# Rows of 272 columns in place of 258 for the first layer's gathered tokens

## What is computed

```
xn = layernorm(x)
x  = x + attention(xn) + ffn(xn)
```

## Time and profile before

| | |
|---|---|
| median of three runs | 1185.54 us |
| lowest, highest | 1183.62, 1187.75 us |
| profiled execution, its own time | 1182.18 us |
| its span, first to last instruction | 1180.4 us |
| mean granted TensorE clock | 0.956 |
| PE, DVE, ACT, POOL busy | 87%, 65%, 51%, 27% |
| share of the 16 DMA engines, queue of SP | 24.5% |
| the same, queue of POOL | 7.2% |

### The profile page before, as it was taken

How to read it: one execution, slowest core, us unless ns; L and a number is a source line. 1 busy time by engine, 2 the same in 40 slices (tenths; PEclk the granted TensorE clock), 3 DMA queues, 4 the chain that set the end, 5 groups by cost and what they waited for, 6 DMA issues and landing times.

```text
span 1180.4 us, 17538 instructions
## 1 busy us (share of the span) xinstructions
PE 1031.3 (87%) x5780; PEld 744.3 (63%) x5780; DVE 764.5 (65%) x1591; ACT 606.1 (51%) x911; POOL 317.1 (27%) x331
## 2 busy tenths in 40 slices
PE   4979697578999938699998999999999997999996
PEld 3867576467999924455454555555555555888885
DVE  6585254446665525789888878888888837444438
ACT  6325244246555543356665665666656665544431
POOL 2003678125674420000000011221221000455442
PEclk9999899789999969799999999999999998999999
DMA  6862233344444354012111113221222206333243
GB/s 229 311 269 81 94 110 123 104 130 128 154 128 130 117 213 143 7 31 33 17 29 27 27 48 61 54 64 41 59 59 59 65 3 204 100 106 106 86 183 147
DMA packets 49140, 120.49 MB, mean 102 GB/s; under 512 B 7752, under 2 KB 24904, under 8 KB 48520
## 3 DMA queue, kind: packets, MB, share of 16 engines
q1 hardware_dynamic: 36096, 82.80, 24.5%
q0 software_dynamic: 11808, 32.37, 7.2%
q10 hardware_dynamic: 1152, 4.19, 0.9%
HBM read 72.30 MB, written 52.42 MB: 106 GB/s over the span
## 4 chain that ended last, share of the span: by engine, by line
PE 69%; DVE 16%; issue 4%; ACT 4%; DMA 3%; another core or an unknown queue 2%; POOL 1%; SPq 0%; ACTq 0%; DVEq 0%; POOLq 0%
PE psum L812 11%; PE psum L833 9%; PE psum L821 6%; PE psum L539 5%; PE psum L541 5%; PE psum L625 4%; DVE work_f L1690 4%; PE psum L540 4%; PE psum L626 4%; PE psum L627 4%; PE psum L611 2%; PE psum L636 2%; DVE x L1305 1%; PE psum L848 1%
## 5 line engine op out<-in xcount | busy, mean ns | idle before, releaser
L1690 DVE TENSOR_REDUCE work_f<-psum 128x1 f32<-128x512 f32 x512 | 335.5, 685 | 66.8 <-PE psum L812 60.0
L1198 ACT ACTIVATE work_f<-psum 128x1024 f32<-128x1024 f32 x256 | 252.9, 1025 | 122.6 <-PE psum L821 85.5
L812 PE MATMUL psum<-work_r 128*128 128x512 f32 x512 | 201.4, 445 | 24.4 <-DVE work_f L1690 9.5
L476 POOL DMA_INDIRECT yk<-yb,dest x134 | 131.3, 980 | 243.9 <-ACT yb L1052 211.9
L812 PEld LDWEIGHTS psum<-work_r 128*128 128x128 f32 x512 | 92.1, 190 | 148.3 <-DVE work_f L1690 57.6
L821 PE MATMUL psum<-qm,work_r 128*128 128x512 f32 x512 | 163.5, 401 | 1.2 <-ACT work_f L1198 1.2
L469 POOL DMA_INDIRECT xg<-xn,slot x112 | 108.3, 967 | 188.3 <-PE psum L848 150.2
L833 PE MATMUL psum<-work_f 128*32 128x512 f32 x1024 | 131.6, 608 | 0.6 <-ACT work_f L1198 0.5
L625 PE MATMUL psum<-wexp,xbh 128*128 x268 | 102.6, 383 | 7.5 <-issue 7.5
L821 PEld LDWEIGHTS psum<-qm,work_r 128*128 128x128 f32 x512 | 91.6, 189 | 21.5 <-ACT work_f L1198 8.3
L626 PE MATMUL psum<-wexp,xbh 128*128 x268 | 96.4, 360 | 0.0
(11 more groups left out here) (215 smaller groups left out, 2011.4 us busy)
## 6 DMA issues: line engine op xcount, KB each, us to landing
xb<-xg SPq DMA_DIRECT2D x67, 258.0 KB
xg<-in_pad SPq DMA_DIRECT2D x1, 10320.0 KB
yg<-yk SPq DMA_DIRECT2D x20, 512.0 KB, 9.0
stage<-in_moe SPq DMA_DIRECT2D x16, 608.0 KB
xg<-in_pad SPq DMA_DIRECT2D x1, 7224.0 KB
work_r<-work_r SPq DMA_DIRECT2D x128, 48.0 KB
work_r<-work_r SPq DMA_DIRECT2D x32, 192.0 KB
stage<-in_moe SPq DMA_DIRECT2D x16, 384.0 KB, 4.0
```

The lines of the kernel that those rows point to most:

```text
L476: nc.gpsimd.indirect_dma_start(yk[l], bass.IndirectOffsetOnAxis(ap=dest[:, j % 8, i:i + 1], axis=0), yb[l][:, j % 2, i, :], None).then_inc ...
L812: nc.tensor.matmul(next_bank(pe, ("scores", n), b_mx, n + 1), qs[g % 2][:, t * P:(t + 1) * P], km[g % 4][:, r, :], start=True, stop=True). ...
L1198: nc.scalar.activation(pt[t % 2][:, 2 * h:2 * h + 2, :], psum[:, 3 + 2 * h:5 + 2 * h, :], ACT.Exp, scale=float(HD) ** -0.5).then_inc(b_ex, 1)
L1690: v.reduce_max(mx[:, s % 2, i:i + 1], ring["scores", n], AX.X).then_inc(b_mx, 1)
```

## The change

A row of layer 0's table gets 272 columns (1088 bytes, 17 times 64) in place of 258; a row of layer 1's keeps 258. `HX` becomes a pair of widths, one for each layer. The 14 further columns of `xn[0]` are set to zero once, by a GpSimd memset at the start. The input `pad` gets 272 columns for both layers, so layer 1's fill reads the first 258 of each 272. `xn[0]` and the buffers in its area are wider, and the areas ahead of them start 128 columns earlier.

```diff
-HX = H + 2
+HX = (H + 16, H + 2)
@@
-        rt0, xt0, aw0, work0 = M + 2304, M + 10880, M + 19072, M + 23232
-        stg0, xn0 = M + 38608, M + 42256
+        rt0, xt0, aw0, work0 = M + 2176, M + 10752, M + 18944, M + 23104
+        stg0, xn0 = M + 38480, M + 42128
@@
-        xn = [place(f"xn{l}", c, [P, TT, HX]) for l, c in enumerate((xn0, xn1))]
+        xn = [place(f"xn{l}", c, [P, TT, HX[l]]) for l, c in enumerate((xn0, xn1))]
@@
-        xb = [place(f"xb{l}", a, [P, 2, 2, HX]) for l, (a, c) in enumerate(two)]
-        xbh = [place(f"xbh{l}", a + 1032, [P, 2, 2 * KH, P], f32r) for l, (a, c) in enumerate(two)]
+        xb = [place(f"xb{l}", a, [P, 2, 2, HX[l]]) for l, (a, c) in enumerate(two)]
+        xbh = [place(f"xbh{l}", a + 4 * HX[l], [P, 2, 2 * KH, P], f32r) for l, (a, c) in enumerate(two)]
@@
-        xg = [nc.dram_tensor(f"xg{l}", (ROWS[l], HX), f32, kind="Internal").ap() for l in range(2)]
+        xg = [nc.dram_tensor(f"xg{l}", (ROWS[l], HX[l]), f32, kind="Internal").ap() for l in range(2)]
@@
                 sp.dma_start(xg[l].rearrange("(n p) h -> n p h", p=PAD),
-                             pad_in[l * PAD:(l + 1) * PAD, :].unsqueeze(0).broadcast_to([n, PAD, HX])).then_inc(m_init, 16)
+                             pad_in[l * PAD:(l + 1) * PAD, 0:HX[l]].unsqueeze(0).broadcast_to([n, PAD, HX[l]])).then_inc(m_init, 16)
@@
             nc.gpsimd.memset(zero[:, 1:2], -0.5).then_inc(s_zero, 1)
-            pool.wait_ge(s_zero, 2)
+            nc.gpsimd.memset(xn[0][:, :, H + 2:HX[0]], 0.0).then_inc(s_zero, 1)
+            pool.wait_ge(s_zero, 3)
@@
-                v.tensor_copy(share[:, j % 8, :], xb[l][:, j % 2, :, H + 1:HX].rearrange("p n o -> p (n o)")).then_inc(m_ix, 1)
+                v.tensor_copy(share[:, j % 8, :], xb[l][:, j % 2, :, H + 1:H + 2].rearrange("p n o -> p (n o)")).then_inc(m_ix, 1)
@@
-    pad = zeros(2 * PAD, HX)
+    pad = zeros(2 * PAD, HX[0])
```

More of the change, by code:

```diff
@@ L110, in program @@
         two = ((xn0, M + WE0 * E0), (on1, M + 21504))
-        hidden = (xn0 + 3080, on1 + 3080)
-        xb = [place(f"xb{l}", a, [P, 2, 2, HX]) for l, (a, c) in enumerate(two)]
-        xbh = [place(f"xbh{l}", a + 1032, [P, 2, 2 * KH, P], f32r) for l, (a, c) in enumerate(two)]
-        xbl = [place(f"xbl{l}", a + 2056, [P, 2, 2 * KH, P], f32r) for l, (a, c) in enumerate(two)]
+        hidden = (xn0 + 4 * HX[0] + 2048, on1 + 4 * HX[1] + 2048)
+        xb = [place(f"xb{l}", a, [P, 2, 2, HX[l]]) for l, (a, c) in enumerate(two)]
+        xbh = [place(f"xbh{l}", a + 4 * HX[l], [P, 2, 2 * KH, P], f32r) for l, (a, c) in enumerate(two)]
+        xbl = [place(f"xbl{l}", a + 4 * HX[l] + 1024, [P, 2, 2 * KH, P], f32r) for l, (a, c) in enumerate(two)]
         sgb = [place(f"sgb{l}", a, [P, 2, F1]) for l, a in enumerate(hidden)]
```

## The result

The changed kernel takes 1201.91 us (median of four, 1199.99 to 1202.24) where the kernel before takes 1184.81 beside it: a ratio of 1.0136, interval 1.0116 to 1.0155, 17.1 us slower. The forecast of no measurable change was wrong, and the time lies outside its range of 1181 to 1197 us. The rival that was given 0.18, the fill in small pieces, named 1200.8 us, and its marks are all in the trace.

What follows compares the result with a forecast made beforehand. TensorE, busy 87% of the span, was taken to bound the kernel. Memset, scatter and pair loads cost 0; fills ending 8.1 us later (2.1 + 6.0) hid under 13.4 us of cover, giving 1185.5 us, range 1181 to 1197.

Steps and rivals of the forecast that it cites:

- no measurable change: Whole kernel: the later fill stays covered, cost 0, 1185.5 us; chance 0.74.
- the fill in small pieces: Slower rival, layer 1's fill: 94 ns a piece, expert 0 lands 30.6 us late, 1200.8 us; chance 0.18.
- Where the change acts: Layer 1's fill breaks into 7168 pieces of 1032 bytes, delaying experts 0 to 2 queued behind it; fill +6.0 us.
- the marks to look for: Some 7000 more DMA packets; ACT's first expert 0 step stays at 104.7 us, or starts later if the slower rival holds.
- The price of a piece: Layer 1's fill: about 50 ns a piece, bounded by 45.9 (scatter writes) and 58.7 (pair loads), so 25.6 us.
- the prediction's own sum: Start of layer 0's attention: 2.1 + 512 X - 19.6 us of delay against 13.4 + 1.9 of cover; X is a piece's time.
- Fill of layer 0: Its 20 copies carry 5.4% more bytes on ten engines: +2.1 us on 39.1 us.
- The covers: Expert 0's weights land 13.4 us before ACT takes them; 1.9 us more behind ACT, before PE's transposes.
- Rows of 1088 bytes: Layer 0's memset, scatter and pair loads: cost 0; by the skill page aligning makes a row 2% longer.
- The estimate for small pieces: Layer 1's fill by the skill page's fixed packet cost: 36/33 of 19.6, or 21.4 us.
- The faster rival: Layer 0's scatter: aligned rows remove DVE's unnamed 13.0 us wait, saving PE 10.1 us, 1175.4 us; chance 0.08.
- The chances: No measurable change 0.74, the fill in small pieces past 71 ns 0.18, the faster case 0.08.

Runs made afterwards that it cites:

- e1: Changed kernel with a contiguous padding input of its own (258 columns) for layer 1; 1183.34 us, ratio 0.9999 to the kernel before.
- e2: Kernel before with layer 1's padding rows 272 columns apart, so its fill breaks into 7168 pieces of 1032 bytes; 1195.53 us, ratio 1.0101.
- e3: Changed kernel with layer 1's fill issued behind the weights of experts 0 to 2, on its own semaphore; 1181.84 us, ratio 0.9986.
- e5: Changed kernel with 272 columns in both tables and layer 1's padding rows 288 columns apart; 1157.60 us against 1155.72, ratio 1.0011.
- e9: Changed kernel, unaltered, timed once more on a third chip; 1173.16 us against 1157.65 for the kernel before, ratio 1.0131.
- e7: Kernel before with a third transfer of 7224 KB in large packets behind the two fills; 1164.11 us against 1155.72, ratio 1.0072.
- e6: Kernel before with nine copies behind its end, one at a time; 14 copies of 1024-byte pieces at destination pitch 1032 took 52.8 us.
- e8: Kernel before with six DRAM to DRAM copies behind its end; 14 copies of 1040-byte pieces at pitch 1088 took 41.6 us.

## Why the prediction was wrong, step by step

- **Where the change acts: right.** That layer 1's fill, which the change doesn't name, is where it could cost, what queues behind it, and the marks to look for all came out; e1 and e2 show it from both sides and e3 shows that the queue's order is the path.
- **The price of a piece: the step that failed.** It took about 50 ns, between 45.9 and 58.7 from the nearest rows, and 86.6 was measured. Neither row could bound it. The scatter writes such rows, but in bursts of 8 for an engine every 1.27 us, at a mean share of 0.29, and the pair loads only read. The fill writes without a pause from ten engines and more, and that is where pieces off a 32-byte unit become dear (3 copies 53 ns, 10 copies 78, 14 copies 111). A price read under light use is no upper bound for heavy use. By the prediction's own sum 86.6 ns give 2.1 + 44.3 - 19.6 - 15.3 = 11.5 us, or 1197.0 us; the rest is the next term.
- **Fill of layer 0: right alone, mis-sized beside the pieces.** +2.1 us was +2.7 in e1. In the changed kernel it ended at about 82 us, and in e1, 19.6 us before the fill's end at 92.5, at 73: 9 us more. The prediction put what layer 1's pieces do to it at nothing, without a reason. While layer 0's fill has ten engines, the others work on the pieces, and all move less. The same window of the kernel before and of e5, to be set beside the 215 GB/s of the changed kernel:

```profile
40.00:56.00 16.00, 16.00 (x94) 13.98 (x94) 10.14 (x52) 4.78 (x8) 0.00 (x0) 1.00 0.79 303
```
```profile
40.00:56.00 16.00, 16.00 (x94) 14.03 (x93) 10.15 (x52) 4.77 (x8) 0.00 (x0) 1.00 0.83 304
```

e1 has 302 GB/s there, e2 247 and e9 252. As an estimate, four engines of pieces at 86.6 ns move 48 of the 215 GB/s, which leaves 167 for ten engines that move 275 alone. So it is the pieces off a unit that hold the large packets up, and not small pieces as such.

- **The sum as it was.** Expert 0 was there at 127.96, 36.7 us later than the 91.3 of the prediction: 2.7 for the bytes, 9 for the contention, 24.4 for layer 1's fill (44 us from 82 to 126, against 19.6), together 36.1. Less 13.4 of cover, the 36.7 leave 23.3 at ACT, which is what the timeline shows.
- **The covers: right.** 13.4 us ahead of ACT; behind it I had 1.9 us, and it was 2.9 here (23.3 at ACT, 20.4 at PE), and 2.9 again in e7 and in e9. Another 2.6 us come back here by the end of the span, from what is not known. The rival's 1200.8 us is close to 1201.9 partly by luck: its 94 ns were too many, and the contention was left out.
- **Rows of 1088 bytes: right.** The memset, scatter, pair loads and waits cost nothing, within the 0.15% of e1. The Trainium skill, page DMA: Bandwidth & Descriptors, section How a descriptor splits into AXI transactions, speaks of reads from the 256-byte boundary below. For copies of 1024-byte pieces it would make, as an estimate, 36.3 beats with a source pitch of 1032 and 34 with one of 1152; they took 49 and 51 ns, on two chips, so no such price shows, and the large one is on the write side. (For the rows of the change the count by the Trainium skill's page is 37 against 36.5 beats, so 1% and not the prediction's 2.)
- **The estimate for small pieces.** The Trainium skill, page DMA: Bandwidth & Descriptors, section Why small descriptors are slow (HBM only), gave 21.4 us for layer 1's fill, 9% above large packets. For pieces on whole units the copies agree in kind (26.2 us for 1024 bytes against 24.4 for large packets, 7%), for the others they don't (55.1 us).
- **The faster rival fell.** With layer 0's rows aligned the waits for an unnamed release stay; in the changed kernel, 96 to 260 us:

```profile
ACT work_r L994 <- remote: 16.9, 5, 7.2
...
DVE x L1307 <- remote: 11.5, 1, 11.5
```

They are missing in e6 and e8, where all rows have 1032 bytes, and in e5 and e9, where they don't. So they go with the chip and not with the rows.

- **The chances.** The mechanism had no row of its own, and a transfer of a kind that the trace does not contain deserved more than 0.18.

## What to carry to other kernels

When an edit changes a shared input's width, look at every transfer that reads it: one that was a contiguous stretch may fall into thousands of pieces, and what counts is what queues behind it. Lay out rows that many DMA engines write to DRAM at a pitch of whole 32-byte units; here that was worth a factor of two in the copies (55.1 against 26.4 us), of 1.6 in a piece of the fill (86.6 against 55 ns), and nothing in the light traffic of scatters and loads. And bound an unseen transfer by rows of the same load, not only of the same size.

## What the runs showed of the hardware

- Pieces near 1 KB that end or start inside a 32-byte unit of DRAM were written at 5.8 to 7.7 ns a piece by 10 to 14 engines that all read the same 512 rows, where pieces on whole units went at 3.5 to 3.7. With 3 engines there was no difference (53 ns on each, against 54 to 56 for pieces on whole units), and 16 engines that read rows of their own went at 4.2. Whether the engines, the source rows or the places written make that, is open.
- Such pieces on some engines also hold up large packets on the others: 303 GB/s in 40 to 56 us of the kernel before, 215 in the changed one, 304 in e5 with pieces on whole units.
- Large packets from DRAM to DRAM took 1.63 us for 44 KB with ten engines at work and 1.91 with 14.
- The same program is quicker on some chips than on others: the kernel before took 1183.2, 1155.7 and 1157.7 us on three. In the profiles of the quicker ones the waits without a named releaser, 33.8 us of them on DVE and ACT in the first trace, are missing. What they are, and whether they make the difference, stays open.
